# A graph layer and a ternary FFN on one core: one compare on GpSimd, output rows through the degrees' bank, six banks and six turned rows

## What is computed

```python
xn    = layernorm(x)
agg   = segment_sum(xn[src], dst); deg = segment_sum(1, dst)
h     = xn @ W_self + b_self + (agg / max(deg, 1)) @ W_neigh
h     = layernorm(h) * gamma + beta;  h = where(h >= 0, h, alpha * h)
x1    = x + (h + xn)
# weights: scale = mean(|w|) per group of 128 + 1e-5
#          wq = clip(round(w / scale), -1, 1) * scale          (-1, 0 or 1 times scale)
y     = layernorm(x1)
out   = x1 + (silu(y @ wq_gate.T) * (y @ wq_up.T)) @ wq_down.T
```

## Time and profile before

| what | value |
|---|---|
| median of 3 runs | 1559.13 us (1558.26 to 1559.78) |
| the profiled execution, device time | 1556.55 us |
| its span (first to last instruction) | 1554.8 us |
| mean granted TensorE clock | 0.993 |
| busy: TensorE / VectorE / ScalarE / GpSimd | 1483.5 / 1074.3 / 1141.7 / 947.8 us |
| end of the table stage (first gather) | 232.75 us |
| last steps of the FFN | about 1543 us |

### The profile page before, as it was taken

The page is one execution under the profiler, slowest core; times in us unless marked ns, Lnnn a source line. Parts: engine busy times, 40 slices in busy tenths (PEclk is TensorE's granted clock), DMA queues, the critical chain, the costliest instruction groups (busy, mean ns, idle before and its releaser), DMA issues.

```text
span 1554.8 us, 21492 instructions
## 1 busy us (share of the span) xinstructions
PE 1483.5 (95%) x6421; PEld 764.6 (49%) x6422; DVE 1074.3 (69%) x2336; ACT 1141.7 (73%) x1986; POOL 947.8 (61%) x936
## 2 busy tenths in 40 slices
PE   6889998999998999999999999999999999999997
PEld 3434444454654555555555455555555545554443
DVE  7899963565767476675766756757666666675975
ACT  3434430102988979899797888988989989999886
POOL 2211217776777777777777777777777777773000
PEclk9999999999999999999999999999999999999999
DMA  8967639899888888998888888888888878884100
GB/s 299 261 183 247 190 109 335 297 307 323 247 265 224 251 248 254 256 238 241 242 251 252 229 242 221 270 245 242 244 227 249 239 227 237 229 258 125 35 21 33
DMA packets 210384, 353.37 MB, mean 227 GB/s; under 512 B 104986, under 2 KB 104986, under 8 KB 210258
## 3 DMA queue, kind: packets, MB, share of 16 engines
q0 software_dynamic: 70560, 231.27, 52.0%
q1 hardware_dynamic: 139708, 120.73, 26.0%
HBM read 295.79 MB, written 39.62 MB: 216 GB/s over the span
## 4 chain that ended last, share of the span: by engine, by line
PE 74%; DVE 10%; issue 4%; POOL 4%; ACT 4%; DMA 3%; SPq 0%; DVEq 0%; ACTq 0%; POOLq 0%
PE f_ps L931 19%; PE f_ps L932 19%; PE f_ps L772 14%; PE agg_ps L846 10%; PE agg_ps L848 10%; POOL rows L724 4%; ACT f_ps L1008 2%; DMA xnt_rows<-work 2%; PE f_ps L876 1%; DVE st6p L1084 1%; DVE work L1340 1%; DVE hsx L1190 1%; DVE scl L1184 1%; DVE acc L1359 1%; DVE hsx L1189 1%
## 5 line engine op out<-in xcount | busy, mean ns | idle before, releaser
L724 POOL DMA_INDIRECT rows<-node_table,idx x882 | 896.6, 1017 | 302.5 <-issue 275.7
L1008 ACT ACTIVATE f_ps<-f_ps,ratio 128x512 f32<-128x512 f32 (+2 forms) x1303 | 775.0, 677 | 113.5 <-PE f_ps L932 107.2
L931 PE MATMUL f_ps<-x1T,tern 128*128 128x512 f16 (+2 forms) x1144 | 416.1, 368 | 21.5 <-DVE work L1340 13.5
L932 PE MATMUL f_ps<-x1T,tern 128*128 128x512 f16 (+2 forms) x1144 | 415.6, 367 | 0.0
L846 PE MATMUL agg_ps<-rows,hot 128*128 128x512 f16 x846 | 323.2, 382 | 4.6 <-DMA rows<-node_table,idx 3.6
L848 PE MATMUL agg_ps<-rows,hot 128*128 128x512 f16 x846 | 321.1, 380 | 0.0
L1359 DVE SCALAR_TENSOR_TENSOR acc<-f_ps,scl,acc 128x512 f32<-128x512 f32 (+2 forms) x143 | 102.2, 715 | 192.9 <-PE f_ps L932 125.7
L931 PE MATMUL f_ps<-hT,tern 128*128 128x512 f16 (+2 forms) x572 | 208.2, 367 | 3.2 <-DVE work L1340 2.8
L932 PE MATMUL f_ps<-hT,tern 128*128 128x512 f16 (+2 forms) x572 | 208.1, 367 | 0.0
L931 PEld LDWEIGHTS f_ps<-x1T,tern 128*128 128x128 f16 x1144 | 112.1, 98 | 135.9 <-DVE work L1340 21.2
L846 PEld LDWEIGHTS agg_ps<-rows,hot 128*128 128x128 f16 x846 | 119.5, 141 | 113.8 <-issue 31.5
(11 more groups left out here) (165 smaller groups left out, 1624.7 us busy)
## 6 DMA issues: line engine op xcount, KB each, us to landing
rows<-node_table,idx POOLq DMA_INDIRECT x882, 4.7
hsx<-own_rows SPq DMA_DIRECT2D x49, 256.0 KB, 3.9
hsx<-in_x SPq DMA_DIRECT2D x48, 256.0 KB, 5.1
out_nodes<-work SPq DMA_DIRECT2D x48, 256.0 KB, 4.0
node_table<-work SPq DMA_DIRECT2D x30, 256.0 KB, 3.3
xnt_rows<-work SPq DMA_DIRECT2D x26, 256.0 KB, 5.9
xj<-xnt_rows SPq DMA_DIRECT2D x26, 256.0 KB, 4.9
acc<-own_rows SPq DMA_DIRECT2D x23, 256.0 KB, 5.7
```

Of the source, the lines that this page charges most:

```text
L724: pool.indirect_dma_start(out=rows[:, j, :], out_offset=None, in_=table[:, :], in_offset=bass.IndirectOffsetOnAxis(ap=of[:, j:j + 1], axis ...
L931: pe.matmul(to, lhs, parts[0], start=g == 0, stop=False, skip_group_check=True)
L932: pe.matmul(to, lhs, parts[1], start=False, stop=True, skip_group_check=True).then_inc(p_ff, 1)
L1008: act.activation(ps, ps, ACT.Copy, scale=ratio[:, w if up else 2, j:j + 1]).then_inc(a_scaled, 1)
```

## The change

Four things change. (1) Of a weight tile's two compares VectorE keeps the second; it makes `half` (0.5 x scale, 128x4) instead of the first, and GpSimd makes the first as four 128x128 `tensor_scalar` operations ahead of its subtraction. Loads and evictions that reuse the weights' place wait for GpSimd's subtraction instead of VectorE's compare. (2) The table stage has YB = 6 banks and XTR = 6 ring slots; the three new slots lie in `rows`, the gathers' buffer, so the first gather also waits for all stores of turned rows. The product of block 0 stands ahead of the transposes of block 1. (3) The output rows of blocks 0 to 44 leave the lanes: they are transposed into the degrees' bank, now `side_ps`, at ticks 11 and 16 of a slot (2, 6, 10 and 14 after slot 48), and added three ticks later. The plan has 1804 steps instead of 1849, which moves the chunks' first steps. (4) Of the last chunk's four down sums VectorE evicts two.

```diff
-    OUT_FROM, OUT_EVERY = 0.1, 0.45
 ...
-                if held_sums and held_sums[1] == "down" and held_sums[2:] == (1, 1):
-                    outs_left += [(pos + OUT_FROM + OUT_EVERY * j if held_sums[0] < CHUNKS - 1 else 0, FIRST[held_sums[0]] + j)
-                                  for j in range(SIZE[held_sums[0]])]
+                if held_sums == (CHUNKS - 1, "down", 1, 1):
+                    outs_left += range(FIRST[-1], BLOCKS)
 ...
+    room = [(t, k) for t in range(BLOCKS + 8) for k in ((11, 16) if t < BLOCKS else (2, 6, 10, 14))]
+    for c in range(CHUNKS - 1):
+        for j in range(SIZE[c]):
+            while room[0] <= AT_OF[LAST_DOWN[c] + 4]:
+                room.pop(0)
+            t, k = room.pop(0)
+            TURN_AT[t, k] = FIRST[c] + j
+            ADD_TICK[t + (k + 3) // TICKS, (k + 3) % TICKS] = FIRST[c] + j
 ...
-        XTR = 3
-        xnT_ring = [work[:, 3 + i].rearrange("p (k n) -> p k n", k=KT) for i in range(XTR)]
+        XTR = 6
+        xnT_ring = [tile.rearrange("p (k n) -> p k n", k=KT) for i in range(3) for tile in (work[:, 3 + i], rows32[:, 15 + i])]
 ...
-        YB = 4
+        YB = LANES
 ...
-                    sp.wait_ge(v_cmp, (w - 1) * FT + (hi - 1) // KT + 1)
+                    sp.wait_ge(pool_tern, (w - 1) * FT + (hi - 1) // KT + 1)
 ...
+                w, i = divmod(n, FT)
+                for g in range(KT):
+                    over = pool.tensor_scalar(wcmp[:, n % 2, 0, g], wstage[:, i * KT + g, :], half[:, n % 2, g:g + 1], None, ALU.is_gt)
+                over.then_inc(pool_cmp, 1)
+                pool.wait_ge(pool_cmp, n + 1)
                 pool.tensor_tensor(wtern[:, n % WTR], wcmp[:, n % 2, 0], wcmp[:, n % 2, 1], ALU.subtract).then_inc(pool_tern, 1)
 ...
             pool.wait_ge(a_xn, BLOCKS)
+            pool.wait_ge(p_y, BLOCKS)
 ...
+            for i in range(XTR):
+                pool.wait_ge(st_xt[i], 16 * len(range(i, len(LATER), XTR)))
 ...
             turn0(0)
             for i in range(BLOCKS):
-                if i + 1 < BLOCKS:
+                if 0 < i < BLOCKS - 1:
                     turn0(i + 1)
 ...
+                if i == 0:
+                    turn0(1)
 ...
+                after(pe, v_out, turned_back[0])
+                pe.matmul(side_ps[:, 0:1], degs[:, :], ones[:, 0:1], start=True, stop=True).then_inc(p_deg, 1)
 ...
+                if c < CHUNKS - 1:
+                    pe.wait_ge(a_dn, KT * (c + 1))
+
+                    after(pe, v_out, b)
+                    pe.wait_ge(v_inv, degrees)
+                    turned_back[0] = b + 1
+                else:
+                    pe.wait_ge(a_dn, KT * c + 2)
+                    pe.wait_ge(v_dn, 2)
 ...
+                    if (t, k) in TURN_AT:
+                        turn_out(TURN_AT[t, k], min(t + 1, BLOCKS))
 ...
+                dve.tensor_scalar(half[:, n % 2, :], scale, 0.5, None, ALU.mult)
                 over = scale[:, :, None].broadcast_to((P, KT, P))
-                dve.scalar_tensor_tensor(out=wcmp[:, n % 2, 0], in0=over, scalar=0.5, in1=tile, op0=ALU.mult, op1=ALU.is_lt)
 ...
+                elif kind == "down" and c == CHUNKS - 1 and w:
+                    dve.wait_ge(p_ff, s + 1)
+
+                    dve.wait_ge(p_t4, FIRST[c])
+                    dve.tensor_scalar(yT[:, 2 * i + w, 0:width], ps, scl[:, 2, j:j + 1], None, ALU.mult).then_inc(v_dn, 1)
 ...
+                    if (t, k) in ADD_TICK:
+                        add_out(ADD_TICK[t, k])
```

61 lines of the change are left out of this document (33 added, 28 removed).

## The result

The changed kernel takes 1586.85 us in the median of 4 runs (1585.59 to 1590.21) against 1558.7 us for the kernel before beside it: ratio 1.0178, 95% interval 1.0162 to 1.0194. It is 28 us slower, where 1552 us and 7 us faster had been forecast; the time lies above the range. Both signs of being wrong that the prediction named are there: the first gather starts after 232 us, and the waits for x1 behind 600 us make over 16 us.

The account below looks back on a forecast made before the run. TensorE was taken as the bound nearly everywhere, VectorE in the table stage. Terms -5 - 11.9 - 7.6 + 3 + 4 + 8 + 1.7 + 1.5 - 0.5 = -6.8 us took 1559.13 to 1552 us, range 1547 to 1557.

Parts of the forecast that it names:

- Both signs of being wrong: First gather before 222 or after 232 us, or waits for x1 behind 600 us under 4 or over 16 us.
- it fits: Table stage: GpSimd's four compares at 0.29 us make a tile 2.3 us, against a block of 3.87 us.
- Rival 3: GpSimd is dear: 1567 us at 1.15 us a compare, or 1558 if edge operations wait behind subtractions; chance 0.08.
- Hindrance: Table stage: VectorE waiting behind GpSimd's SBUF reads costs 0.4 us, one overlap by a third of a subtraction.
- The gate: Table stage: scale of blocks 21 to 27 remains the limit; block 20's product 4.6 us earlier, stage wins 5 us.
- Six banks and six turned rows: Table stage: waits for stores of turned rows go; waits for low halves, such as 2.38 and 1.38 us, go or shrink.
- Lanes: Main stage: TensorE's 15 waits for output-block additions go, winning 11.9 us before 1416 us and 7.6 behind.
- The side bank's own waits: Main stage: 3 us for transposes waiting on the ratio of degrees, 4 us for additions after slot 48.
- Chunks' first steps: Main stage: earlier first steps wait for x1 0.4, 0, 0.8, 6.0 and 1.2 us, 8 in all; last chunk 1.5.
- the landing: Main stage: transposes of x1 land 3 us after issue, 11.6 us behind the degrees' matmul (bounds 10.0 and 13.5).
- The low clock: Main stage: TensorE's lower clock behind the long wait for x1 in slot 42 costs 1.7 us.
- Rival 4: Main stage: x1 lands 15 us behind the degrees' matmul, first steps cost 31 us instead of 9.7, 1573 us; chance 0.07.

Follow-up runs that it names:

- compare_two_of_four: Changed kernel, but GpSimd compares two of a tile's four 128x128 parts and VectorE the other two in one operation; 1577.67 us, ratio 1.0139.
- first_compare_left_out: Kernel of wait_later_3, but nobody makes a tile's first compare and GpSimd subtracts the second from itself; 1557.18 us, ratio 1.0009.
- wait_later_3: Changed kernel with both compares on VectorE and TensorE's wait for the table stage's last evictions behind the look at the edge overflow; 1567.57 us, ratio 1.0058.
- both_mended_2: Kernel of wait_later_3 with chunks' first steps at the earliest two ticks later, one place per chunk empty, turns at ticks 1 and 11; 1556.03 us, ratio 0.9979.
- all_mended: Kernel of both_mended_2 with VectorE's edge range operations two blocks later; ratio 0.9979.
- rings_alone: Kernel before the change with only six banks, six turned rows and the new order of block 0; 1558.8 us, ratio 1.0007.
- compare_one_of_four: Changed kernel, but GpSimd compares one of a tile's four parts and VectorE three; ratio 0.9957, read only by its first gather at 238.18 us.
- gpsimd_compare_alone: Kernel before the change with only GpSimd's four-part first compare and its waits for the weights' place; 1582.18 us, ratio 1.0168.
- weights_asked_later: Changed kernel with SyncE's loads of weights two blocks later; ratio 1.0056, first gather at 250.3 us.

## Why the prediction was wrong

- **Where GpSimd's price comes in.** "With four compares at the former a tile takes 2.3 us, and tiles come at most one a block, 3.87 us; it fits." This step failed twice. The compare takes 0.59 us, within the stated bounds but twice the value taken from the 128x128 operation of the earlier trace rows. And "it fits" compared a tile with a block and left out GpSimd's pauses, which the trace of before has too (5.92 + 0.66 + 7.53 us around the all-reduce at 123.02). At 2.4 us a tile, the forecast's own price, the stage loses 11.6 us (compare_two_of_four). Of all this 18.5 us (233.90 to 252.41) are in the result, the largest part of the 35 us between forecast and measurement. Rival 3, GpSimd as the slower one, came nearest, but its condition did not hold: it wanted 0.68 us a compare or more and put 15 us at 1.15, and 24 us (first gather at 252.4 instead of 228) came at 0.59 to 0.67. By the table even one compare a tile, four times less than the change gives GpSimd, costs 4.3 us. A chance of 0.08 was far too low for a price that no row showed.
- **Hindrance.** The 0.4 us for it was too little, but small beside the rest. It goes both ways: L1224 took 1.65 us instead of 0.69 at 40.11, beside GpSimd's subtraction begun at 40.06, and four compares 4.55 instead of 2.35 us at 75.97 under VectorE's L1180. The Trainium skill has the rule ("SBUF — State Buffer", "Who interferes with whom"): a VectorE instruction with two SBUF inputs contends with a GpSimd instruction that reads SBUF, and the order of issue decides which of them waits; both rows agree. The compares' mean above their least time, 75 ns in 132, is 9.9 us of GpSimd, an upper bound for what it lost so.
- **The gate.** "The gate that is left is the scale of blocks 21 to 27" holds under the forecast's own condition, a compare that costs nothing (first_compare_left_out): the size was too small, the first gather came at 224.4 where 228 had been forecast, since that scale came 6 us earlier than before and not 3. What the forecast lacked is the gates right behind it: with both compares on VectorE TensorE waits another 0.6 (wait_later_3) to 1.8 us (both_mended_2) for the scale of blocks 35 to 41, and when the first gate moved by 5 us, 4 us of them were spent at the scale of blocks 28 to 34 (all_mended). In the changed kernel none of these counts: behind 116 us the chain goes through GpSimd.
- **Six banks and six turned rows** took the small waits away and let one pause grow, as forecast; the 0.6 us at the first gather (rings_alone) are not clear of noise. That the wait for the last evictions moved ahead of the look at the overflow wasn't priced: 2.1 us and a low clock ahead of slot 0 (rings_alone), mostly given back within slot 0.
- **Lanes.** Right: the 16.3 us of the earlier trace rows are gone in every kernel with the side bank. The side bank's own waits were forecast at 3 + 4 us and measured at 0.6 + 5.8.
- **Chunks' first steps.** Place and order were right (slots 14, 38, 42, 46 and the last chunk), and the issue ends 8.2 to 8.9 us behind the degrees' matmul as said. The term that was mis-sized is the landing: 3 us taken, 5.3 to 6.6 measured in slots 14, 42 and 46, though 2.9 in slot 38. The waits are 2.8, 0, 0.5, 8.9, 3.6 us and 1.7 for the last chunk, 17.6 in all, where 8 + 1.5 stand in the sum. The earlier trace rows had 4.9 us at 505.54, set aside as a late gather's. The low clock behind them and behind the side bank's wait costs 6.8 us instead of 1.7. These two terms are 13 us; the main stage came out 9.6 us above its forecast (+7.8 instead of -1.8). Part of the difference is in waits for gathers, 3.1 us instead of 4.8 before; the rest is not accounted for. Rival 4's condition, 15 us behind the degrees' matmul, nearly held (14.3, 14.7, 14.2).

## What to carry to other kernels

Before work is moved to an engine with room, write down its pauses and who may run ahead of it by how much: an engine that is busy 60% of the time between two pauses of 15 us still stops its neighbours if the buffer between them holds two items. A gate is found by moving it, and one that moves for nothing has another right behind it: list the later waits for the same engine, however short (here 0.6 us behind one of 9.9), before a gain at the longest is put into the sum. Where a plan moves a consumer towards its transfer, take the longest landing of the trace, not the median of another transfer; here even that, 4.9 us, was less than the 6.6 measured.

## What the runs showed of the hardware

GpSimd's two all-reduces between tiles have a pause on both sides, and in most traces it waits there for nothing that the profile shows. Ahead of the one at 116 to 130 us it is 5.8 to 6.3 us in 13 of the 19 traces, 7.5 and 7.8 us in rings_alone and compare_one_of_four, and 9.5 to 10.3 us in the four kernels in which GpSimd makes two or four parts of every compare (after, gpsimd_compare_alone, compare_two_of_four, weights_asked_later). What makes it longer was not tried. Ahead of the one at 189 to 221 us it is 5.7 to 6.6 us in all. Behind either, the next tile starts 6.7 to 8.0 us later, or up to 9.4 where a transpose lands last. The Trainium skill gives about 6 us for the first call to a freshly loaded kernel ("GPSIMD Engine Reference", "Instruction dispatch"); the pause ahead is of that size in most traces, and no row shows what is done in it.

A 128x128 compare (`tensor_scalar`, float32 to float16) takes GpSimd 0.59 us at the least, twice the 0.29 us of an operation of that size in the earlier trace rows, and half the 1.15 us of a subtraction on four times as many elements.

What stays open: why the transposes of x1 land 2.9 us behind their issue in slot 38 and up to 6.6 in slot 42 (3.0 to 6.6 there in five traces of the same plan), and why slot 4 takes 27.2 to 35.0 us from one execution to the next.
